# A two-layer graph attention kernel on one core: its row gathers also wait for the query products of the third step behind

## The chip, the cores and the metric

One NeuronCore of a Trainium2 chip runs the whole kernel. The metric is the device time of one execution in microseconds (us). The median of three runs of the kernel before is 5051.74 us, the runs lie between 5045.22 and 5057.14 us.

## The reference, cut to what matters

The input is a graph of 6250 nodes (256 features each) and 200000 edges that are sorted by their destination `dst`. Two layers of graph attention follow one another, each with a residual and a layer norm. In each layer the rows of the source nodes are gathered per edge, a score is formed with the query of the destination node, a softmax runs over all edges of a destination, and the weighted rows are summed per destination.

```python
# layer 0: 4 heads of 32, x[6250,256]; e comes from edge_attr[200000,64]
kj    = k[src] + e
alpha = einsum('ehc,ehc->eh', q[dst], kj) * scale
expa  = exp(alpha - segment_max(alpha, dst)[dst])
alpha = expa / (segment_sum(expa, dst)[dst] + 1e-16)
out   = segment_sum((v[src] + e) * alpha[..., None], dst)
...
# layer 1: one head of 256, with an edge weight added to the score
scores  = sum(q[dst] * k[src], axis=-1) * scale + (edge_weight[:, None] @ we + be)[:, 0]
...
out     = segment_sum(v[src] * attn[:, None], dst)
x       = layer_norm(x + out + linear(x, ws, bs), g1, b1)
```

## The kernel before, in words

The program has five phases with a barrier between them: node projections (n0), the edge phase of layer 0 (L0), node work (n1), the edge phase of layer 1 (L1), node work and the feed-forward part (n2). The change touches the two edge phases alone.

**Steps, pairs, chunks.** The edges are cut into `NS` = 391 steps of 512 edges (4 tiles of 128). Destinations are cut into 49 windows of 128 nodes. A (step, window) combination that has edges is a pair; there are 439, and the program runs 440 (the last is padding). Since the edges are sorted, most steps have one pair, and 48 steps have one more, so a step has 1.12 pairs on average. Eight pairs are a chunk; there are 55. A step's source rows are gathered once and used by all its pairs. Which pair is the first of a step is not fixed at build time: a table `start_tab` that the kernel computes tells, for each step, how many pairs lie ahead of it. POOL loads it eight entries at a time into registers (`load_row`, L264).

**POOL (`gathers`, L622 to L640)** issues the gathers: per step four indirect DMAs, each 128 rows of 1 KB, into one of `SLOTS` = 16 slots of the tile `rows`. Ahead of a step's gathers it waits for three things: that DVE has scored all pairs of all steps up to the fifth behind (`LEAD` = 5, semaphore `score`), that the slot's former rows have been used up (`summed`, that is `msg` in L0 and `agg` in L1), and that the gathers of the step two before have landed. A wait against a register is followed by an increment of a semaphore `gate` (`stand_by`, L61); the two make one instruction, attributed to L67.

**SP** loads the edge attributes (L0) and counts landed steps: `tell_landed` (L490) waits for a pair's gathers and raises `landed`, for which DVE waits in `add_edges` (L1009, layer 0, the first use of the rows) or in `dots` (L1033, layer 1).

**PE** forms, per pair, the edge part (`edge_keys`, operands `w_c` and `ea`, layer 0), the queries of the 512 edges (`queries`, operands in the tile `place`), and, a chunk behind, the weighted sums (`back`: `msg` and `oh` in layer 0, `rows` and `oh` in layer 1). All its matmuls carry the helper's line L1377. Queries lie in two alternating parts of PSUM, so the queries of pair g wait until pair g-2 is scored. PE raises the semaphore `q` once per pair:

```python
after(pe, s["score"], g - 1)                  # L1437: pairs up to g-2 are scored
queries_ready(c, st)
...
if L is L0 or st == 1:
    i.then_inc(s["q"], 1)                     # L1445
...
if st != 1:                                   # bias_products, layer 1
    i.then_inc(s["q"], 1)                     # L1455
```

In layer 1 the signal thus comes behind the four small `bias_products` of the pair (`128x3` outputs). For the third pair of a chunk they stand behind `shrink_first`, the end of the softmax work of the chunk before (L1525 to L1527), while the queries themselves stand ahead of it.

**DVE** scores a pair (`products` L1016 and `scores_of` L1021 in layer 0, `dots` L1033 in layer 1), and does the masked scans, the messages (L1149 in layer 0), its half of the weights (L1154 in layer 1) and the accumulation (L1174) of the chunk before in between. The scans stand at the head of a chunk. **ACT** makes the one-hot operands in `place` (L738, L743) and `oh`, and issues the loads of `dst_row` and of the node blocks (L725, L730).

Of the kernel before, what the change touches and what calls it, by code (L numbers as in the profile page):

```python
# [43 lines left out]
LEAD = 5  # L44
# [10 lines left out]
def after(eng, sem, value):  # L55

    if not (isinstance(value, int) and value <= 0):
        eng.wait_ge(sem, value)


def stand_by(eng, gate, sem, value):  # L61

    if isinstance(value, int):
        after(eng, sem, value)
    else:
        eng.wait_ge(sem, value)
        eng.sem_inc(gate, 1)  # L67


def build(nc, a, out):  # L70
    ctx = ExitStack()
    with ctx:
# [3 lines left out]
        def sem(name):  # L76
            return ctx.enter_context(nc.semaphore(name))
# [186 lines left out]
        def load_row(engine, ap, low=None, top=None, because=None):  # L264

            return nc.values_load_multi_w_load_instructions(ap, engines=[engine], min_val=low, max_val=top,  # L266
                                                            skip_runtime_bounds_check_because=because)[1]
# [13 lines left out]
        def slots(name):  # L281
# [8 lines left out]
                  q=sem("n1_qT"), qc=sem("n1_qT_copied"), qk=sem("n1_qk"), high=sem("n1_high"), low=sem("n1_low"), split=sem("n1_split"))  # L290
# [284 lines left out]
        def _(pool):  # L575
# [44 lines left out]
            gate = sem("pool_gate")  # L620

            def gathers(L):  # L622
                s = L.s
                summed = s["msg" if L is L0 else "agg"]
                starts = {}

                for t in range(NS):
                    if t % 8 == LEAD - 1:
                        k = t - LEAD + 1
                        starts.update(zip(range(k, k + 8), load_row(ENGINE.Pool, start_tab[0:1, k:k + 8], 0, NPAIR)))  # L630
                    if t >= LEAD:
                        stand_by(pool, gate, s["score"], starts[t - LEAD + 1])
                    if t >= SLOTS:
                        stand_by(pool, gate, summed, starts.pop(t - SLOTS + 1))
                    after(pool, s["gathered"][t % 2], 64 * (t // 2))
                    for j in range(JT):
                        pool.indirect_dma_start(  # L637
                            out=L.rows[:, t % SLOTS, j, 0:D], out_offset=None, in_=L.table,
                            in_offset=bass.IndirectOffsetOnAxis(ap=src_all[:, t * JT + j:t * JT + j + 1], axis=0))\
                            .then_inc(s["gathered"][t % 2], 16)  # L640

            def root(norm):
# [6 lines left out]
                return stage  # L649

            gathers(L0)
            end_phase(pool, 2)
            def n1_split(w, b, k):
# [7 lines left out]
            pool.memset(x1_rows[:, :, :, D], 1.0)  # L661
            pool.drain()
            gathers(L1)
            end_phase(pool, 4)

# [1016 lines left out]
```

## Time and profile before

| | us |
|---|---|
| median of three runs | 5051.74 |
| lowest, highest | 5045.22, 5057.14 |
| span of the profiled execution | 6753.4 |
| of it: n0, L0, n1, L1, n2 (windows) | 107, 2998, 303, 2957, 389 |
| busy: PE, DVE, POOL, ACT | 4299.6, 3831.3, 3308.1, 3003.4 |

The profiled execution has only its span; no time of its own beside it is given. It is 1702 us longer than the median of the runs without the profiler. A row of instructions reads: start, duration, engine, line, operation, tile written <- tiles read, and in brackets how long the engine was idle before it and what ended that. "remote" or "another core or an unknown queue" is a wait whose releaser the profile does not name. A busy time holds instructions alone; between two gathers POOL is not counted as busy.

### The profile page before, as it was taken

The page shows a single profiled execution, that of the slowest core. Times are in us where ns is not written, and L with a number is a line of the kernel's source. Part 1 is how long each engine was busy: PE and PEld are TensorE (multiplying, and loading weights), DVE is VectorE, ACT ScalarE, POOL GpSimd, SP SyncE. Part 2 cuts the span into 40 slices and gives each one's busy share as a digit, 9 for nine tenths or more (in the row PEclk, how much of TensorE's full clock was granted, in tenths as well). Part 3 has the DMA queues.
Part 4 walks back from the last instruction along what each step waited for, and adds up shares of the span by engine and source line. Part 5 has one row for each costly group of instructions (what it writes and reads, how often), then busy time and mean ns, then how long its engine had stood idle before and what let it go on. Part 6 is the DMA issues. An engine that isn't in the chain of part 4 may idle for free.

```text
span 6753.4 us, 105844 instructions
## 1 busy us (share of the span) xinstructions
PE 4299.6 (64%) x23291; PEld 3492.8 (52%) x23291; DVE 3831.3 (57%) x12902; ACT 3003.4 (44%) x6997; POOL 3308.1 (49%) x3637
## 2 busy tenths in 40 slices
PE   6555555565565566566746666666666666666698
PEld 3454554555455555454534555555554555554587
DVE  4565665666566666666734444455454444444588
ACT  1444454555454454554324444444444444444432
POOL 2545555455555455452355545554555554454355
PEclk8777777777777777777978778787888787777899
DMA  6555555555555555553446556565666665555422
GB/s 201 148 145 148 146 145 146 145 153 148 149 152 145 145 152 154 148 148 99 122 141 163 161 153 162 157 162 157 164 160 158 160 160 158 157 163 158 125 73 70
DMA packets 774181, 996.11 MB, mean 147 GB/s; under 512 B 189569, under 2 KB 559489, under 8 KB 773553
## 3 DMA queue, kind: packets, MB, share of 16 engines
q10 hardware_dynamic: 394272, 443.81, 23.8%
q0 software_dynamic: 150224, 410.39, 22.7%
q1 hardware_dynamic: 229056, 135.14, 7.5%
q8 instruction: 198, 3.24, 0.2%
q14 instruction: 431, 3.52, 0.2%
HBM read 862.98 MB, written 125.90 MB: 146 GB/s over the span
## 4 chain that ended last, share of the span: by engine, by line
another core or an unknown queue 22%; PE 21%; DVE 17%; issue 16%; DVEq 7%; ACTq 5%; ACT 5%; DMA 2%; POOL 2%; SPq 1%; POOLq 1%
PE ps L1377 20%; DVE rows L1009 2%; DVE score L1021 2%; DVE prod L1033 2%; ACT oh L750 2%; DVE acc L1174 2%; DMA acc_d<-acc 2%; ACT place L738 1%; ACTq L827 1%; DVE prod L1016 1%; DVEq L1233 1%; ACTq L730 1%; SPq L266 1%; DVEq L1231 1%
## 5 line engine op out<-in xcount | busy, mean ns | idle before, releaser
L637 POOL DMA_INDIRECT rows<-kv_d,src_all x1564 | 1535.2, 982 | 1543.1 <-DVE score L1021 951.0
L637 POOL DMA_INDIRECT rows<-x_d,src_all x1564 | 1487.0, 951 | 1450.5 <-DVE prod L1033 962.3
L1377 PE MATMUL ps<-place 128*128 128x256 bf16 (+2 forms) x10560 | 1459.9, 288 | 296.4 <-issue 186.8
L1377 PEld LDWEIGHTS ps<-place 128*128 128x128 bf16 (+1 forms) x10560 | 1250.9, 149 | 587.4 <-issue 317.6
L1377 PE MATMUL ps<-rows,oh 128*128 x3520 | 1093.2, 470 | 457.3 <-DVE oh L1154 340.7
L1033 DVE SCALAR_TENSOR_TENSOR prod<-rows,ps 128x256 f32<-128x256 f32 x1760 | 637.3, 418 | 906.8 <-remote 549.9
L1377 PEld LDWEIGHTS ps<-rows,oh 128*128 128x128 f32 x3520 | 797.8, 236 | 617.9 <-issue 478.8
L750 ACT ACTIVATE oh<-iota_row,rel 128x128 f32<-128x128 f32 x2640 | 837.9, 388 | 552.9 <-remote 408.8
L1377 PE MATMUL ps<-msg,oh 128*128 128x132 f32 x3520 | 607.0, 330 | 595.8 <-DVE msg L1149 331.8
L1377 PEld LDWEIGHTS ps<-msg,oh 128*128 128x128 f32 x3520 | 544.1, 235 | 638.9 <-DVE msg L1149 421.0
L738 ACT ACTIVATE place<-dst_row,node_tab 128x512 f32<-128x512 int32 (+1 forms) x880 | 613.2, 708 | 385.4 <-DVE acc L1174 145.3
L757 ACT ACTIVATE oh<-oh,prob,prob_neg 128x128 f32<-128x128 f32 x880 | 374.2, 484 | 801.7 <-remote 466.4
L743 ACT ACTIVATE place<-place,ones 128x512 f32<-128x512 f32 (+1 forms) x880 | 635.0, 722 | 184.7 <-issue 115.5
L1009 DVE TENSOR_TENSOR rows<-rows,ps 128x1024 f32 x440 | 537.3, 1221 | 176.8 <-issue 95.9
L1377 PE MATMUL ps<-w_c,ea 128*128 128x256 f32 x1760 | 610.4, 482 | 34.9 <-issue 23.5
L1016 DVE TENSOR_TENSOR prod<-rows,ps 128x512 f32<-128x512 f32 x440 | 299.8, 681 | 555.3 <-remote 503.3
L1174 DVE SCALAR_TENSOR_TENSOR acc<-acc,keep_tab,ps 128x132 f32<-128x132 f32 (+1 forms) x770 | 318.7, 414 | 508.2 <-remote 279.3
L1377 PEld LDWEIGHTS ps<-w_c,ea 128*128 128x128 f32 x1760 | 391.6, 246 | 89.7 <-issue 26.2
L789 ACT ACTIVATE pen_r<-ps 128x128 f32<-128x128 f32 (+1 forms) x110 | 30.0, 272 | 813.6 <-remote 337.8
L1021 DVE TENSOR_REDUCE score<-prod 128x16 f32<-128x512 f32 x440 | 301.9, 686 | 44.7 <-issue 10.8
L1149 DVE TENSOR_TENSOR msg<-rows,prob 128x512 f32<-128x512 f32 x440 | 293.3, 687 | 1.6 <-issue 1.3
L762 ACT ACTIVATE oh<-oh,ones 128x1024 f32<-128x1024 f32 x275 | 268.9, 978 | 19.2 <-issue 0.3
(217 smaller groups left out, 4152.9 us busy)
## 6 DMA issues: line engine op xcount, KB each, us to landing
dst_row<-in_dst_row ACTq DMA_DIRECT2D x880, 256.0 KB
place<-q_d ACTq DMA_DIRECT2D x440, 192.8 KB
acc_d<-acc ACTq DMA_DIRECT2D x440, 128.5 KB
ea<-in_ea SPq DMA_DIRECT2D x440, 128.0 KB
acc_d<-acc ACTq DMA_DIRECT2D x440, 66.0 KB
place<-q_d ACTq DMA_DIRECT2D x440, 64.0 KB
rows<-kv_d,src_all POOLq DMA_INDIRECT x1564
rows<-x_d,src_all POOLq DMA_INDIRECT x1564
```

Of the source, the lines that this page charges most:

```text
L637: pool.indirect_dma_start(out=L.rows[:, t % SLOTS, j, 0:D], out_offset=None, in_=L.table, in_offset=bass.IndirectOffsetOnAxis(ap=src_all[: ...
L738: act.activation(L.oht[st % PLACES], dst_row[st % PLACES][:, :], ACT.Abs, scale=-1.0, bias=node_tab[:, bass.ds(g, 1)])
L743: act.activation(L.oht[st % PLACES], L.oht[st % PLACES], ACT.Relu, scale=-1.0, bias=ones[:, 0:1])\
L750: act.activation(oh[:, st % OHS, j, :], iota_row[:, :], ACT.Abs, scale=-1.0, bias=rel[par][:, st, j:j + 1])
L757: i = act.activation(o, o, ACT.Relu, scale=prob_neg[par][:, n:n + 1], bias=prob[par][:, n, 0:1])
L1009: v.tensor_tensor(kv, kv, e_ps(b).rearrange("p (j n) -> p j n", j=JT).unsqueeze(2) .to_broadcast([P, JT, 2, DM]), ALU.add).then_inc(s["add ...
L1016: v.tensor_tensor(half, held(kv_rows, slot[CH * c + st])[:, :, 0:DM], q_ps(L, st % 2).rearrange("p (j n) -> p j n", j=JT), ALU.mult)
L1021: v.tensor_reduce(score[par][:, st * JT:(st + 1) * JT, :], prod[:, :, st % 2 * DM:(st % 2 + 1) * DM] .rearrange("p j (h n) -> p j h n", h= ...
L1033: i = v.scalar_tensor_tensor(out=prod[:, j, :], in0=x1[:, j, 0:D], scalar=1.0, in1=q_ps(L, b)[:, j * D:(j + 1) * D], op0=ALU.mult, op1=ALU ...
L1149: v.tensor_tensor(m, held(kv_rows, slot.pop(g))[:, :, DM:2 * DM].rearrange("p j (h c) -> p j h c", h=HEADS), prob[par][:, st * JT:(st + 1) ...
L1174: v.scalar_tensor_tensor(acc[st % ACCS][:, 0:L.AW], old[:, 0:L.AW], keep_tab[:, bass.ds(g, 1)], agg_ps(L, b), ALU.mult, ALU.add).then_inc( ...
L1377: return pe.matmul(out_, lhsT=lhsT, rhs=rhs, start=first, stop=last)
```

## The change: one more wait ahead of each step's gathers

From step 5 on, POOL also waits until `q` has reached the number of pairs that lie ahead of step t-2, that is, until PE has signalled the query products of all pairs of all steps up to t-3. The wait stands between that for `score` and that for the slot. So that the table entry t-2 is in a register by then, each block of eight entries is loaded two steps earlier.

```diff
                 for t in range(NS):
-                    if t % 8 == LEAD - 1:
-                        k = t - LEAD + 1
+                    if t >= LEAD - 3 and (t - LEAD + 3) % 8 == 0:
+                        k = t - LEAD + 3
                         starts.update(zip(range(k, k + 8), load_row(ENGINE.Pool, start_tab[0:1, k:k + 8], 0, NPAIR)))
                     if t >= LEAD:
                         stand_by(pool, gate, s["score"], starts[t - LEAD + 1])
+                        stand_by(pool, gate, s["q"], starts[t - LEAD + 3])
                     if t >= SLOTS:
                         stand_by(pool, gate, summed, starts.pop(t - SLOTS + 1))
                     after(pool, s["gathered"][t % 2], 64 * (t // 2))
```

On POOL, at steps 3 to 7 of layer 0, the order before. A row `L637 DMA ... [waits ...]` is the first gather of a step with the semaphores waited for since the row ahead; the row behind it holds the other three gathers. `l0_gathered0` and `l0_gathered1` are the landings of even and odd steps.

```order
L637 DMA rows<-kv_d,src_all 128x256 [waits l0_gathered1]
L637 DMA rows<-kv_d,src_all 128x256 x3
L266 TENSOR_LOAD start_tab
L266 ISA x16
L637 DMA rows<-kv_d,src_all 128x256 [waits l0_gathered0]
L637 DMA rows<-kv_d,src_all 128x256 x3
L637 DMA rows<-kv_d,src_all 128x256 [waits l0_score,l0_gathered1]
L637 DMA rows<-kv_d,src_all 128x256 x3
L637 DMA rows<-kv_d,src_all 128x256 [waits l0_score,l0_gathered0]
```

And the order after the change, on POOL at steps 2 to 6 (the gathers' line is now L638):

```order
L266 TENSOR_LOAD start_tab
L266 ISA x16
L638 DMA rows<-kv_d,src_all 128x256 [waits l0_gathered0]
L638 DMA rows<-kv_d,src_all 128x256 x3
L638 DMA rows<-kv_d,src_all 128x256 [waits l0_gathered1]
L638 DMA rows<-kv_d,src_all 128x256 x3
L638 DMA rows<-kv_d,src_all 128x256 [waits l0_gathered0]
L638 DMA rows<-kv_d,src_all 128x256 x3
L638 DMA rows<-kv_d,src_all 128x256 [waits l0_score,l0_q,l0_gathered1]
L638 DMA rows<-kv_d,src_all 128x256 x3
L638 DMA rows<-kv_d,src_all 128x256 [waits l0_score,l0_q,l0_gathered0]
```

The table load moved two steps up and `l0_q` stands in each later step; no gather changed its place among the others, and the other engines' programs are the same.

## Rows read from the trace of the kernel before

**Rows 1.** The page's first two lines: span, and busy time of each engine.
```profile
span 6753.4 us, 105844 instructions
...
PE 4299.6 (64%) x23291; PEld 3492.8 (52%) x23291; DVE 3831.3 (57%) x12902; ACT 3003.4 (44%) x6997; POOL 3308.1 (49%) x3637
```
**Rows 2.** The page's chain of waits, shares of the span by engine.
```profile
another core or an unknown queue 22%; PE 21%; DVE 17%; issue 16%; DVEq 7%; ACTq 5%; ACT 5%; DMA 2%; POOL 2%; SPq 1%; POOLq 1%
```
**Rows 3.** Busy time by phase: window, length, each engine's busy time, clock, DMA share, GB/s.
```profile
0.00:107.00 107.00, 82.96 (x246) 46.22 (x246) 59.47 (x199) 11.37 (x28) 13.60 (x67) 0.97 0.77 228
107.00:3105.00 2998.00, 1729.37 (x9137) 1516.66 (x9138) 1832.43 (x3947) 1493.61 (x3452) 1535.17 (x1564) 0.75 0.54 148
3105.00:3408.00 303.00, 207.15 (x993) 151.03 (x991) 204.28 (x903) 110.84 (x363) 79.51 (x148) 0.88 0.36 101
3408.00:6365.00 2957.00, 1949.46 (x10944) 1490.27 (x10945) 1426.00 (x6804) 1269.09 (x2824) 1487.01 (x1564) 0.80 0.59 159
6365.00:6754.00 389.00, 330.71 (x1976) 288.58 (x1973) 309.10 (x1052) 118.52 (x331) 192.80 (x294) 0.96 0.24 71
```
**Rows 4.** The page's costliest groups: busy, mean ns, idle before and its releaser.
```profile
L637 POOL DMA_INDIRECT rows<-kv_d,src_all x1564 | 1535.2, 982 | 1543.1 <-DVE score L1021 951.0
L637 POOL DMA_INDIRECT rows<-x_d,src_all x1564 | 1487.0, 951 | 1450.5 <-DVE prod L1033 962.3
...
L1033 DVE SCALAR_TENSOR_TENSOR prod<-rows,ps 128x256 f32<-128x256 f32 x1760 | 637.3, 418 | 906.8 <-remote 549.9
```
**Rows 5.** POOL on the tile rows: gathers' ns min/median/max, and who ended POOL's idle time.
```profile
L637 POOL DMA_INDIRECT rows<-kv_d,src_all x1564: 942/949/1462, 107.4 to 3099.0; - x196
...
  DVE prod L1033: 962.3, 259
  DVE score L1021: 951.0, 183
...
  DVE msg L1149: 7.8, 1
```
**Rows 6.** Timeline of POOL in L1: last gather of step 161, first three of step 162.
```profile
4609.27 0.95 POOL L637 DMA_INDIRECT rows<-x_d,src_all  x1 [0.30 <-issue]
4616.64 0.95 POOL L637 DMA_INDIRECT rows<-x_d,src_all  x1 [6.42 <-DVE prod L1033]
4617.89 0.94 POOL L637 DMA_INDIRECT rows<-x_d,src_all  x1 [0.30 <-issue]
```
**Rows 7.** Timeline of DVE in L1: last dot of pair 176, first of 178, first of 182.
```profile
4615.33 0.42 DVE L1033 SCALAR_TENSOR_TENSOR prod<-rows,ps 128x256 f32<-128x256 f32 x1
...
4628.34 0.42 DVE L1033 SCALAR_TENSOR_TENSOR prod<-rows,ps 128x256 f32<-128x256 f32 x1 [5.66 <-remote]
...
4650.86 0.42 DVE L1033 SCALAR_TENSOR_TENSOR prod<-rows,ps 128x256 f32<-128x256 f32 x1 [5.55 <-remote]
```
**Rows 8.** Timeline of PE in L1: queries of 178, shrink, then bias products of 178.
```profile
4618.89 1.95 PE L1377 MATMUL ps<-place 128*128 128x256 bf16 x12 [0.93 <-ACT place L743]
...
4622.73 0.58 PE L1377 MATMUL ps<-shrink_d,first_oh 1*128 1x1 f32 x2 [1.45 <-issue]
4623.25 2.94 PE L1377 MATMUL ps<-place 128*128 128x3 bf16 x20
```
**Rows 9.** Timeline in L0: score 203, POOL's step 186, messages, queries of 205, use in pair 209.
```profile
1530.18 0.69 DVE L1021 TENSOR_REDUCE score<-prod 128x16 f32<-128x512 f32 x1
...
1531.75 0.95 POOL L637 DMA_INDIRECT rows<-kv_d,src_all  x1 [3.81 <-DVE score L1021]
...
1532.85 0.68 DVE L1149 TENSOR_TENSOR msg<-rows,prob 128x512 f32<-128x512 f32 x1
1533.00 1.35 POOL L637 DMA_INDIRECT rows<-kv_d,src_all  x1 [0.30 <-issue]
...
1533.42 1.39 PE L1377 MATMUL ps<-place 128*128 128x128 f32 x8
...
1557.63 1.22 DVE L1009 TENSOR_TENSOR rows<-rows,ps 128x1024 f32 x1 [0.29 <-issue]
```
**Rows 10.** Direct DMAs of the size of one gather: KB each, us from issue to landing.
```profile
rows<-x_d SPq DMA_DIRECT2D x98, 128.0 KB, 2.1
...
kv_d<-rows ACTq DMA_DIRECT2D x49, 128.0 KB, 2.8
```
**Rows 11.** POOL's register waits (line L67): ns min/median/max.
```profile
L67 POOLq EVENT_SEMAPHORE  x1522: 4/17/737, 138.9 to 6338.6; - x191
```

## The prediction

> **What bounds the kernel now.** I read the page's span and busy times first. The span is 6753.4 us, and no engine is busy for more than 64% of it [rows 1]. That span is 1701.7 us above the median of 5051.74 us. The chain of waits puts 22% of the span, 1486 us, on a releaser that the profile cannot name [rows 2]. It is of the size of the difference. In layer 1 such pauses show as DVE idle for 5.66 and 5.55 us before its dots, ended by "remote" [rows 7]. I take them to be mostly a matter of the profiled execution, so the trace is slower than the kernel that is timed, and a margin read from it must be cut down.
>
> The windows by phase come next [rows 3]. Outside the edge phases lie 107 + 303 + 389 = 799 us. If these are the same without the profiler, each edge phase takes about (5052 - 799) / 2 = 2127 us there, which is 2127 / 391 = 5.44 us per step and 2127 / 440 = 4.83 us per pair.
>
> Then POOL. Inside a step, gathers start 1.25 us apart (4616.64 and 4617.89), of which 0.30 is a gap that is not counted as busy [rows 6]. With that gap, POOL needs 1535 + 1564 x 0.30 = 2004 us in L0 and 1487 + 469 = 1956 us in L1 [rows 3, 4]. PE needs 1949 us in L1 and DVE 1832 us in L0 [rows 3]. So POOL, half idle by the page, is the most loaded engine of both phases: 3960 of 4254 us in a run without the profiler. It has 294 us to spare over 782 steps, 0.38 us a step. In the trace nearly all its waiting is for DVE's scores (183 times in L0, 259 in L1) and once for a slot [rows 5]; it is held back by its lead of five steps.
>
> **The change, part by part.**
> - *Added instructions.* 386 waits in each phase, 772 in all. The present kind has a median of 17 ns, and there are 1522 = 2 x (386 + 375) of them [rows 11]. All of them exposed would be 13 us. But POOL's sequencer passes them beside the gather that runs. I count them only where POOL is idle when it comes to them, 442 steps [rows 5], 7.5 us at most; and as that idle time itself is mostly spare, I take 3 us.
> - *The table load.* It moves by two steps, its count stays. SP, PE, ACT and DVE have the same programs. Nothing.
> - *The wait itself.* It is never weaker than the old one. The queries of pair g are signalled only once pair g-2 is scored, and step t-3 ends at least two pairs behind the end of step t-5. So the gathers come later in nearly every step that is now held by a score. By how much, from one place in each phase:
>   - L1, step 162. The score of pair 176 ends at 4615.75 [rows 7] and POOL starts 0.89 us later, at 4616.64 [rows 6]. The queries of pair 178, the last of step 159, are done at 4620.84, but its signal comes with the first bias products from 4623.25 on [rows 8]. With 0.89 us of reaction the gathers would start at about 4624.1, 7.5 us later.
>   - L0, step 186. POOL starts at 1531.75, after the score of pair 203. The queries of pair 205 end at 1533.42 + 1.39 = 1534.81 [rows 9]. The start would be at 1535.7, 3.9 us later.
> - *Who waits for it.* Behind the gathers stands SP's count of landed steps, then DVE. The fourth gather is issued 3 x 1.25 = 3.75 us after the first. The trace has no landing time for a gather. Direct DMAs of its size land 2.1 to 2.8 us after issue [rows 10], and I take 2.8. In L1 the rows would be there at 4624.1 + 6.6 = 4630.7, and are first used at 4650.86 [rows 7], 20 us later. In L0 they would be there at 1542.3 and are used at 1557.63 [rows 9], 15 us later.
> - *Without the profiler.* The pauses are worth 1701.7 / 880 = 1.9 us per pair. In L1 four pairs lie between, 20 - 8 = 12 us are left; in L0 it is six pairs at most, 15 - 12 = 3 us left. A second way: two whole steps lie between the signal and the first use, 2 x 5.44 = 10.9 us. Of these 0.9 + 3.75 + 2.8 = 7.5 us are needed, and 3.4 us are left. So the lead that is taken away was spare, in the mean. A gap of more than some 3 us on PE just ahead of a signal would use it up.
> - *DVE and POOL side by side.* In L0 a gather takes 982 ns in the mean, against 951 in L1 [rows 4], with a median of 949 and a maximum of 1462 [rows 5]. The one of 1.35 us at 1533.00 ran while DVE made messages [rows 9]. The excess over L1 is 1564 x 0.031 = 48 us of POOL's time. A shift by 3.9 us in a pair period of 4.8 us may move gathers onto such instructions or off them. With nothing lengthened POOL gains 48 us; I take 0, as the gathers of a step fill nearly the whole period anyway (4 x 1.25 = 5.0 of 5.44 us).
>
> The Trainium skill, page "SBUF — State Buffer", section "Who interferes with whom", says that a DVE instruction with two SBUF inputs contends with a GpSimd instruction that reads SBUF, and that DMAs as such never contend with a compute engine. The messages have both inputs in SBUF, so the trace agrees with it. By the page the sum would be open by these 48 us in L0, and unchanged in L1.
>
> The sum: 0 + 3 + 0 = 3 us on 5051.74, about 5055.
>
> **The rivals.**
> - *The lead is spare* (forecast). For it: the margins of 3 to 12 us, and POOL's single wait for a slot. It gives 5042 to 5062.
> - *POOL has no time to lose* (slower). POOL has 0.38 us to spare a step. At the head of a chunk DVE and PE do the scans, and the signal of the chunk's third pair stands behind them in layer 1. POOL now sits idle there instead of working ahead, and has to make up for it later at 5.0 us a step against a demand of 5.44, which it cannot do within a chunk of seven steps (7 x 0.38 = 2.7 us) if it loses more than that. It decides where the delay exceeds the 3.4 us that are left. The L0 place exceeds it by 0.5 us, the L1 place by 4.1 us. One such loss in each of the 55 heads of a phase gives 55 x 0.5 = 28 us up to 55 x 4.1 = 226 us. I take 40 us, near the low end, since in the traced L1 place DVE still met its rows 20 us early: 5092. Against it: the same margins.
> - *A better phase* (faster). The gathers now start when PE has its operands, so they are less in the way of loads and of DVE's messages. From 15 us (a third of the excess) to 48 us: 5004 to 5037, I take 5030. For it: POOL is the most loaded engine, so what it gains counts. Against it: nothing shows that the new phase is better than the old. The page's rule named above is this rival's mechanism for layer 0.
> - *The change does nothing*: if POOL lags so far behind without the profiler that no gate ever holds it, both gates are met when it comes to them. 5052. For it: 3960 of 4254 us. Against it: 442 steps held by a score in the trace.
>
> **How the numbers follow.** About 0.2% (10 us) is what a measurement of this kernel can tell from no change. Spare lead 0.37, nothing 0.04, no time to lose 0.36, better phase 0.23. Same: the first two, 0.41. Slower 0.36, faster 0.23. The predicted time is 5055, the likeliest case. The range goes down to 5020, half into the better phase, and up to 5095, a little past my value for the slower rival; about 2 in 10 are left out, mostly above it. As the cases of both signs hold more than the likeliest, its own range stands here too: 5042 to 5062.
>
> **What the profile after would show.** If I am right: POOL's idle time before gathers is ended mostly by PE instead of DVE. Its total is the same within a few per cent, since it issues the same work. DVE's waits on SP (the landed count) don't grow, and the mean gather stays near 982 and 951 ns. If the slower rival holds, DVE's first use of the rows (L1009, L1033) is released by SP more often, at the second to fourth pair of a chunk. If the faster one holds, the mean gather of L0 falls towards 951 ns, or DVE's and PE's waits on the loads shrink. The forecast is wrong if the time leaves 5042 to 5062 us.

## The result: a little slower, 5078.25 us against 5055.24

Seven runs of each kernel were timed on one chip.

| | us |
|---|---|
| before, median (lowest to highest, 7 runs) | 5055.24 (5045.22 to 5063.39) |
| after, median (lowest to highest, 7 runs) | 5078.25 (5066.89 to 5087.49) |
| ratio, 95% interval | 1.0042, 1.003 to 1.0055 |
| profiled execution of after: its time, its span | 5078.96, 5077.2 |

The change costs 0.42%, some 21 us. That is more than the 0.2% that a measurement can tell, and it lies outside the 5042 to 5062 us that I gave to my forecast.

The first surprise is the profiled execution itself. The span of before was 1702 us above its timed runs [rows 1]. The one of after lies 1.8 us below its own time and amid its timed runs. So the profiler doesn't slow this kernel. Before was therefore profiled once more, unchanged, and gave a span of 5059.5 us. I call this the **clean trace** of before, and the one that the prediction read the **paused trace**. All comparisons up to the last experiment are with the clean one.

The page's first two lines of the clean trace of before:

```profile
span 5059.5 us, 105844 instructions
...
PE 3809.0 (75%) x23291; PEld 3120.8 (62%) x23291; DVE 3808.2 (75%) x12902; ACT 3002.8 (59%) x6997; POOL 3302.1 (65%) x3637
```

And of after, with its chain of waits and its two groups of gathers:

```profile
span 5077.2 us, 106616 instructions
...
PE 3828.2 (75%) x23291; PEld 3135.5 (62%) x23291; DVE 3810.1 (75%) x12902; ACT 3001.0 (59%) x6997; POOL 3289.3 (65%) x3637
...
PE 20%; DMA 17%; DVE 15%; ACT 13%; ACTq 13%; issue 13%; DVEq 5%; POOL 3%; POOLq 1%; SPq 0%
...
L638 POOL DMA_INDIRECT rows<-kv_d,src_all x1564 | 1514.1, 968 | 751.4 <-issue 411.9
L638 POOL DMA_INDIRECT rows<-x_d,src_all x1564 | 1490.0, 953 | 606.2 <-issue 433.0
```

No engine is busy for more than 75%, and 22% on an unnamed releaser [rows 2] is gone. The clean trace of before has these two groups with 1532.0 and 1484.3 us, and idle times of 719.5 and 596.5 us. The idle time before gathers thus rose from 1316.0 to 1357.6 us, by 3%. Of both numbers some 938 us are the 3128 gaps of 0.30 us, so what lies above the gaps rose from 378 to 419 us.

Where the time went, by windows that are cut at the first gather and the last accumulation of each edge phase. The clean before (window, length, busy time of PE, PEld, DVE, ACT, POOL, clock, DMA share, GB/s):

```profile
108.00:2317.00 2209.00, 1557.87 (x9295) 1335.20 (x9295) 1843.17 (x4015) 1509.68 (x3520) 1532.01 (x1564) 0.88 0.73 201
2317.00:2575.00 258.00, 177.26 (x833) 124.82 (x833) 173.87 (x833) 86.62 (x294) 79.52 (x148) 0.92 0.40 114
2575.00:4704.00 2129.00, 1684.50 (x11055) 1345.75 (x11055) 1442.09 (x6875) 1289.56 (x2860) 1484.27 (x1564) 0.92 0.82 221
```

After:

```profile
107.00:2327.00 2220.00, 1562.03 (x9295) 1340.20 (x9295) 1842.62 (x4015) 1508.37 (x3520) 1514.06 (x1564) 0.88 0.73 200
2327.00:2585.00 258.00, 178.56 (x833) 125.81 (x833) 176.49 (x833) 86.75 (x294) 78.88 (x149) 0.91 0.40 114
2585.00:4721.00 2136.00, 1698.00 (x11055) 1354.22 (x11055) 1441.46 (x6875) 1288.88 (x2860) 1489.94 (x1564) 0.91 0.84 221
```

L0 is 11 us longer and L1 is 7 us longer; n1 between them is the same. DVE and ACT are busy for the same time or a little less. POOL is busy 18 us less in L0 and 6 more in L1, PE 4 and 14 us more, at a granted clock that is 0.88 in L0 both times. So the loss of L0 is waiting, not work. The clean trace of before also shows how little POOL had to spare: 1532 + 1564 x 0.30 = 2001 of 2209 us in L0.

Who ends POOL's idle time. In the clean before (us, times):

```profile
  issue: 894.4, 2798
...
  DVE score L1021: 168.3, 129
  DVE prod L1033: 101.4, 89
...
  PE ps L1377: 29.6, 58
```

In the kernel after:

```profile
  issue: 845.7, 2635
  PE ps L1378: 333.1, 315
...
  DVE msg L1150: 38.8, 50
...
  DVE score L1022: 17.4, 57
  DVE prod L1034: 11.7, 37
```

These counts are not steps. They hold the ordinary gaps of 0.30 us inside a step too, when an update of such a semaphore happened to fall into one. Counted at the first gather of each step alone, a score ended the idle time at 117 steps in the clean before (239 us; 78 in L0 and 39 in L1), and at 356 steps in the paused trace, where the prediction reads 442 [rows 5]. After the change PE ends it at 141 steps (280 us; 82 in L0 and 59 in L1), and a score at 13 (4 us). In layer 1 the slot's semaphore is raised by PE too: the clean before has 22 such steps, so not all of the 59 are the new wait's.

The first question was whether the rows now come late. I took, for each step behind the fifth, the time from the end of its last gather to DVE's first use of its rows:

| from last gather to first use, us | L0 median (shortest) | L1 median (shortest) |
|---|---|---|
| paused trace of before | 20.2 (8.4) | 29.3 (18.0) |
| clean trace of before | 11.7 (4.0) | 16.4 (2.1) |
| after | 7.9 (2.4) | 8.4 (2.0) |

The change takes 3.8 us in L0 and 8.0 us in L1, as forecast (3.9 and 7.5). A step's last gather packet ends behind its last gather's instruction by a median of 2.7 us in L0 and 3.3 us in L1 in the clean before (2.4 and 3.3 after), and by 3.7 us in L0 and 4.6 us in L1 or more in one step of twenty. So the typical step still has its rows some 5 us early after the change, but the shortest times of the table leave nothing. DVE's waits on SP's landed count, of which late rows are a part, rose from 25.3 + 52.9 to 28.3 + 57.6 us over the program, by 8 us.

### The profile page after: what moved, and what is told of

Its sections match the earlier page's. It is cut to its first block, busy times and chain, and to the rows that moved or that the text cites. A ratio compares the mean times of both kernels' runs of the same rounds, so it can differ in the third digit from the quotient of the medians.

```text
span 5077.2 us, 106616 instructions
## 1 busy us (share of the span) xinstructions
PE 3828.2 (75%) x23291; PEld 3135.5 (62%) x23291; DVE 3810.1 (75%) x12902; ACT 3001.0 (59%) x6997; POOL 3289.3 (65%) x3637
## 3 DMA queue, kind: packets, MB, share of 16 engines
q14 instruction: 436, 3.57, 0.2%
## 4 chain that ended last, share of the span: by engine, by line
PE 20%; DMA 17%; DVE 15%; ACT 13%; ACTq 13%; issue 13%; DVEq 5%; POOL 3%; POOLq 1%; SPq 0%
PE ps L1378 18%; DMA acc_d<-acc 15%; ACT oh L751 7%; ACTq L828 4%; ACT place L739 3%; ACTq L731 3%; DVE rows L1010 3%; ACTq L726 3%; POOL rows L638 2%; DVE score L1022 2%; DVE acc L1175 2%; DVE prod L1034 1%; DMA dst_row<-in_dst_row 1%; DVEq L1234 1%; ACT place L744 1%
## 5 line engine op out<-in xcount | busy, mean ns | idle before, releaser
L638 POOL DMA_INDIRECT rows<-kv_d,src_all x1564 | 1514.1, 968 | 751.4 <-issue 411.9
L638 POOL DMA_INDIRECT rows<-x_d,src_all x1564 | 1490.0, 953 | 606.2 <-issue 433.0
L1378 PE MATMUL ps<-place 128*128 128x256 bf16 (+2 forms) x10560 | 1313.7, 274 | 144.5 <-DVE score L1022 65.0
L1378 PEld LDWEIGHTS ps<-place 128*128 128x128 bf16 (+1 forms) x10560 | 1154.8, 140 | 370.9 <-issue 89.0
L1378 PE MATMUL ps<-rows,oh 128*128 x3520 | 916.7, 411 | 127.3 <-issue 116.3
L1378 PEld LDWEIGHTS ps<-rows,oh 128*128 128x128 f32 x3520 | 683.7, 202 | 230.2 <-issue 134.6
L1378 PE MATMUL ps<-msg,oh 128*128 128x132 f32 x3520 | 506.1, 290 | 231.4 <-DVE msg L1150 129.8
L1378 PEld LDWEIGHTS ps<-msg,oh 128*128 128x128 f32 x3520 | 439.1, 194 | 290.3 <-DVE msg L1150 270.9
L1378 PE MATMUL ps<-w_c,ea 128*128 128x256 f32 x1760 | 541.7, 437 | 25.3 <-DMA ea<-in_ea 21.2
L1378 PEld LDWEIGHTS ps<-w_c,ea 128*128 128x128 f32 x1760 | 346.7, 219 | 68.5 <-issue 22.1
```

What stands on the lines that cost most here:

```text
L638: pool.indirect_dma_start(out=L.rows[:, t % SLOTS, j, 0:D], out_offset=None, in_=L.table, in_offset=bass.IndirectOffsetOnAxis(ap=src_all[: ...
L1378: return pe.matmul(out_, lhsT=lhsT, rhs=rhs, start=first, stop=last)
```

## The experiments

At this point there were three explanations: the added instructions cost their issue time; the rows come late; or POOL, held at the head of a chunk, makes up for it later and its gathers then meet other transfers. Against them stood the chance that all of it is noise of the single traces. The first two groups of kernels were timed against before on a chip each, with 25 and 17 runs of before (medians 5055.62 and 5053.36 us). Spans of single traces scatter by some 10 us, so times are compared by the ratios of the timed runs.

### One more wait of the old kind (e1)

```diff
                         stand_by(pool, gate, s["score"], starts[t - LEAD + 1])
+                        stand_by(pool, gate, s["q"], starts[t - LEAD + 1])
```

The 772 waits are added with a bound that the score's wait implies already, and the table load stays.

> The kernel before with one more register wait per step on the query semaphore, with the value of the score wait (steps up to t-5), so that it is always met once the score is. It has the added instructions and none of the added delay. Theory A (the later start of the gathers costs the time): 5055 us, no change within 0.1%. Theory C (the 772 added instructions cost it): the whole 0.42%, 5076 us.

Measured: 5059.78 us, ratio 1.0012 (1.0001 to 1.0024). The instructions alone cost about 0.12%, 6 us, with an upper end of 12. My term was 3 us with a bound of 13. The traces show why 17 ns was too little for one of them: two such waits stand 0.096 us apart on POOL's sequencer even where both are met, and POOL starts a median of 0.97 us behind the score that frees it in e1, 0.87 in the clean before.

### The change in one layer (e2, e3)

```diff
+                        stand_by(pool, gate, s["q"], starts[t - LEAD + 3]) if L is L0 else None
```

with the table load moved as in the change; in e3 the condition is `L is L1`.

> The new wait in the edge phase of layer 0 alone. Theory A (POOL has too little time to spare for being held later): both phases pay, layer 0 with the shorter delay (3.9 us at the place read) pays less: 5055 + 5 to 10 us. Theory B (the shifted gathers meet other DMAs, above all the stores of the sums, whose landings now stand in 15% of the chain of waits): layer 0 moves less (203 GB/s against 225 in layer 1), so nearly nothing: 5055 to 5059 us.

> The new wait in the edge phase of layer 1 alone. Theory A: most of the loss, 5055 + 13 to 18 us, as the signal of a chunk's third pair is late there by 7.5 us at the place read. Theory B: nearly all of it, 5055 + 19 to 23 us. Theory C: half of it, 11 us, as half of the instructions are here. Together with the run for layer 0 it tells whether the two parts add up to the whole.

Measured: layer 0 alone 5072.99 us, ratio 1.0037 (1.0024 to 1.005); layer 1 alone 5063.76 us, ratio 1.002 (1.0009 to 1.003). The two add up to 0.57% against 0.42% for both, which their intervals allow. Layer 0 seems to carry the larger part, in the traces too (11 of 18 us), though its delay is half that of layer 1; the two intervals overlap. The delay alone is then no measure of the cost. POOL is as loaded in one layer as in the other, 2001 of 2209 us in L0 and 1953 of 2129 in L1, but DVE has 1843 us of work in L0 against 1442.

### The query wait in place of the score wait (e4)

```diff
-                        stand_by(pool, gate, s["score"], starts[t - LEAD + 1])
+                        stand_by(pool, gate, s["q"], starts[t - LEAD + 3])
```

> The kernel after without the old wait for the scores; the query wait alone is at least as strict, since the queries of pair g come after the score of pair g-2. The gathers start when they do in the kernel after, with as many instructions as before. Theory A or B (the later start costs the time): about 5070 us, +0.3%. Theory C (instructions; the implied wait alone measured +0.12%): that part goes, and what is left is +0.3%. If the instructions were all of it: 5055 us.

Measured: 5072.1 us, ratio 1.0036 (1.0023 to 1.0048), with as many instructions as before (105844). So the later start costs by itself, and it is most of the 0.42%.

### One step tighter (e6)

The wait is for all pairs of all steps up to t-2, and the table load moves up by one more step.

```diff
+                        stand_by(pool, gate, s["q"], starts[t - LEAD + 4])
```

> The query wait one step tighter: all steps up to t-2. The gathers start one more step (about 5 us) later. In the trace after, the first use of the rows stands a median of 5.6 us (layer 0) and 8.5 us (layer 1) behind the end of the last gather, and landing takes some 1.5 to 3 us of it. Theory A: now the rows are late in most steps, DVE's waits on the landed count grow from 86 us to several hundred, and the time is 5200 us or more. Theory B: no such waits at the third step, and a further loss of the same size as before, 5095 us, if the rows still come in time.

(For layer 0 the table above has 7.9 us from the last gather to the first use, not 5.6.)

Measured: 5343.59 us, ratio 1.0591 (1.0575 to 1.0606). Here the rows are late. From the list of waits (engine, tile, line <- releaser: us, times, longest) first the clean before, then this kernel:

```profile
DVE prod L1033 <- SPq L495: 52.9, 42, 10.1
```

```profile
DVE prod L1034 <- SPq L495: 460.6, 205, 11.0
...
DVE rows L1010 <- SPq L495: 315.3, 228, 5.5
```

DVE waits for the landed count for 776 us instead of 78, and the kernel is 290 us slower. That is what late rows look like. After the change the same two lines hold 86 us. So late rows are at most a small part of the 21 us.

### Another lead with the old wait alone (e7, e8)

`LEAD = 6` and `LEAD = 4` in the kernel before.

> The kernel before with LEAD = 6: one step more of lead. In the second trace of before POOL is held by a score in 218 of 782 steps for 270 us. If every bit of lead is worth something, this is the mirror image of the change: -0.1 to -0.3%, 5040 to 5050 us. If the lead of five steps is already spare, no change; if gathers that run further ahead meet more of the other DMAs, slower.

> The kernel before with LEAD = 4: the wait is for the scores of all steps up to t-4 instead of t-5, no query wait, no added instruction. The gathers start about one step later than before where a score holds them, a little earlier than in the kernel after. If the lead is what counts, whichever semaphore takes it away: +0.1 to +0.3%, 5060 to 5070 us. If it is the binding to PE's signal: no change, 5055 us.

Measured: LEAD = 6 5054.01 us, ratio 1.0001 (0.9992 to 1.0011); LEAD = 4 5075.35 us, ratio 1.0048 (1.0035 to 1.0061). More lead than five brings nothing, and one step less costs as much as the change. The lead of before was just enough, not more than enough.

### What the traces of this set show together

DVE's waits before the accumulation for the landing of a store of `acc`, and before the first use of the rows, in L0. The rows are from the list of waits of each trace, over L0. The clean before:

```profile
DVE acc L1174 <- DMA acc_d<-acc: 109.0, 51, 3.5
DVE rows L1009 <- SPq L495: 25.3, 32, 11.6
```

Layer 0 alone (e2):

```profile
DVE acc L1175 <- DMA acc_d<-acc: 132.9, 55, 3.8
DVE rows L1010 <- SPq L495: 24.8, 19, 10.7
```

LEAD = 4 (e8):

```profile
DVE acc L1174 <- DMA acc_d<-acc: 95.2, 52, 4.7
DVE rows L1009 <- SPq L495: 51.9, 59, 2.8
```

| L0 | query wait there | DVE for `acc_d`, us | DVE for rows, us |
|---|---|---|---|
| before, e1, e3, e7 | no, or met at once | 109.0, 110.9, 104.9, 106.2 | 25.3, 24.8, 24.9, 24.7 |
| after, e2, e4 | yes | 120.7, 132.9, 124.3 | 28.3, 24.8, 27.1 |
| e8 | no, lead of four | 95.2 | 51.9 |

Four traces without the new wait in L0 lie within 6 us of each other, and all three with it wait 10 to 28 us longer for a store to land. (The traced run of e2, with 132.9, was its slowest, 5094.29 us.) LEAD = 4 loses its time at another place: its rows are late. So a shorter lead can cost at either place.

Where in a chunk? DVE's own time tells it for L0. I cut it at the end of each pair's score and took the mean of the stretches over the chunks. The stretch up to the seventh score is 6.04 to 6.21 us long in the four traces without the wait and 6.35 to 6.55 us in the three with it; the one up to the sixth is 4.43 to 4.45 and 4.49 to 4.51 us. All others agree within 0.04 us. Before against after that is 0.14 + 0.08 us a chunk, some 12 us over the chunks, about the 11 us by which L0 is longer. DVE's busy time in them is the same. All but a few of L0's waits for a store stand in the stretch up to the seventh score, at one accumulation, the sixth of the chunk, which needs the landing of the chunk's second store. In the stretch up to the sixth score DVE waits for rows: 0 to 0.9 us in all in the four traces, 2.6 to 3.9 in the three. So in L0 the time goes to that store for the most part, and to late rows for a small one.

POOL's busy share with its gaps, by the pair of the chunk in L0, is 0.84 at the second pair before and 0.63 after. It is 0.94, 0.95 and 0.89 at the last three before and 0.98, 0.97 and 0.94 after. POOL stands at the head of the chunk, and runs without a pause at its end. There the accumulations and their stores lie. One chunk shows it. POOL and DVE in the timeline of the clean before (the rows between the two blocks, further gathers and other work of DVE, are not shown):

```profile
1238.80 0.94 POOL L637 DMA_INDIRECT rows<-kv_d,src_all  x1 [4.59 <-DVE score L1021]
```

```profile
1258.08 0.35 DVE L1174 SCALAR_TENSOR_TENSOR acc<-acc,keep_tab,ps 128x132 f32<-128x132 f32 x1
1260.75 0.35 DVE L1174 SCALAR_TENSOR_TENSOR acc<-acc,keep_tab,ps 128x132 f32<-128x132 f32 x1 [2.33 <-DMA acc_d<-acc]
```

and the same chunk after:

```profile
1239.62 0.95 POOL L638 DMA_INDIRECT rows<-kv_d,src_all  x1 [4.12 <-PE ps L1378]
```

```profile
1260.18 0.35 DVE L1175 SCALAR_TENSOR_TENSOR acc<-acc,keep_tab,ps 128x132 f32<-128x132 f32 x1
1263.93 0.35 DVE L1175 SCALAR_TENSOR_TENSOR acc<-acc,keep_tab,ps 128x132 f32<-128x132 f32 x1 [3.41 <-DMA acc_d<-acc]
```

The store's wait is 1.08 us longer at this place. The median time from issue to landing of the 440 stores of L0 is 3.29 us in the clean before, 3.29 in e1, 3.30 in e3 and 3.23 in e7; it is 3.32 after, 3.46 in e2 and 3.41 in e4, and 3.19 in e8. For the chunk's second store alone, the one that is waited for, the mean is 3.38 to 3.53 us without the new wait and 3.62 to 3.82 with it (3.57 in e8). In the clean before, the 17 stores with fewer than 20 gather packets begun in the 3 us behind their issue land in 1.66 us in the median, those with 60 to 100 in 3.58. That goes with stores that land later beside gathers. But nearly all of the 17 are the last stores of the phase, where the phase's loads run out too, so the gathers are not singled out.

The Trainium skill, page "DMA: Bandwidth & Descriptors", section "Queues, rings and completion order", says that a DMA's semaphore increment lands only after every earlier write of the same DMA engine, across its queues. The landing times beside gathers are what it leads one to expect, since stores and gathers have different queues; no run here tests it.

This is read from traces and has not been shown by taking the cause away. For layer 1 the stores don't explain it. DVE's waits for `acc_d` there are 114.1 us before and 99.1 after, and those for rows 52.9 and 57.6. e3 has 67.2 for rows. By the pair of the chunk the rows tell one thing: ahead of a chunk's eighth pair DVE waits for them 5.4 to 9.3 us in all in the four traces without the wait in L1 (before, e1, e2, e7), and 11.3 to 17.7 us in the three with it (after, e3, e4). That is of the size of L1's 7 us, but other waits of DVE scatter by as much between these traces, so it is not shown to be the cause.

### More buffers for the stores (f1 to f4)

To take the cause away, `ACCS` was raised from 4 to 8, so that DVE waits for a store that lies eight pairs back (f1 before, f2 after). In f3 and f4 the stores are counted in four semaphores in place of two as well, so that ACT, too, waits for an older one.

```diff
-ACCS = 4
+ACCS = 8
...
-        acc_scaled = sb("acc_scaled", [P, D + 1])
+        acc_scaled = zero_rows
```

f3 and f4 also have:

```diff
-            for x in ("gathered", "stored"):
+            for x in ("gathered",):
...
+        L0.stored = [(n0["store"][b], 48 * turns(b)) for b in range(4)]
+        L1.stored = [(n1["store"][b], 32 * turns(b)) for b in range(4)]
...
-                    after(act, s["stored"][b], 16 * (CH // 2 * c + st // 2))
-                    act.dma_start(window(L.acc_d, g), acc[st % ACCS][:, 0:L.AW]).then_inc(s["stored"][b], 16)
+                    after(act, stored, base + 16 * (CH // 4 * c + st // 4))
+                    act.dma_start(window(L.acc_d, g), acc[st % ACCS][:, 0:L.AW]).then_inc(stored, 16)
...
```

The parts left out make DVE's wait and SP's wait at the end of the phase use the same four semaphores.

> The kernel before with eight buffers for the sums instead of four (the space comes from one tensor less, zero_rows is used twice). DVE then waits for a store eight pairs old instead of four, so its 221 us of waits for acc_d stores go to about 0. ACT still issues a store only when the store two pairs before has landed. If DVE's waits are on the path: faster, 4900 to 5000 us. If ACT's own wait is what holds the chain and DVE's only mirrors it: no change, 5055 us.

> The kernel after with the same eight buffers. Theory B1 (the shifted gathers delay the stores' landings and DVE pays for it, +12 to +24 us in layer 0 in the traces): the change costs only the instructions here, +0.1% against the run with eight buffers before. Theory A (rows late, POOL short of time), or B2 (the cost comes through ACT's store wait): the change costs 0.3 to 0.5% here too.

> The kernel before with eight buffers and four store semaphores: ACT issues a store once the one four pairs before has landed, instead of two. Now neither DVE nor ACT should wait for a store. If the stores' landings bound the kernel at all, this is the fastest so far, 4850 to 5000 us; POOL, busy for 93 to 98% of most pairs, then becomes the limit, at 391 x 2 x 5.0 us and the 797 us outside, about 4800 us. If POOL already is the limit, no change.

> The kernel after with the same two edits. Theory B (any form of store wait is how the change costs time): +0.1% against the same edits before. Theory A: with the stores out of the way DVE and ACT run closer behind POOL, POOL has no time to spare, and holding it at the head of a chunk costs as much as before or more, +0.4% and up.

The measurement went another way than any of these. In this job every run of the unchanged kernel before took 6740.7 to 6790.8 us (23 runs, median 6767.22), with the pauses of its first profile; so the four kernels can be compared with each other only.

| | us | ratio to before |
|---|---|---|
| f1: before, 8 buffers | 6759.11 | 0.9993 (0.998 to 1.0006) |
| f2: after, 8 buffers | 6194.27 | 0.9151 (0.9124 to 0.9178) |
| f3: as f1, four store semaphores | 6753.7 | 0.9983 (0.9967 to 0.9999) |
| f4: as f2, four store semaphores | 6191.5 | 0.9156 (0.9132 to 0.9179) |

The question on the stores is not answered. The buffers and semaphores do next to nothing here (f1, f3), where pauses take up much of the time. But the change itself is worth 8.4% in this condition (f2/f1 0.9164, f4/f3 0.9168), against a loss of 0.42% in the other. The experiments e1 to e3 had run on the same chip in the clean condition. So it belongs neither to the profiler nor to a chip; what sets it is open.

### What the pauses are

From the trace of f1, the page's first line and who ended POOL's idle time on the tile rows:

```profile
span 6752.5 us, 105836 instructions
```

```profile
  DVE prod L1033: 947.5, 255
  DVE score L1021: 931.4, 171
```

The same two views of f2:

```profile
span 6192.5 us, 106608 instructions
```

```profile
  PE ps L1378: 1081.3, 324
...
  remote: 351.8, 139
```

By these lines POOL waits for 1879 us in f1 and for 1433 us in f2. Counted at the first gather of each step it is held by a score at 341 steps in f1, and by PE or an unnamed releaser at 450 in f2, so f2 is held more often and for a shorter time.

A pause from near, in the paused trace of before, in the timeline, a little ahead of [rows 9]: POOL's gathers, PE's products, then DVE and ACT.

```profile
1524.49 0.94 POOL L637 DMA_INDIRECT rows<-kv_d,src_all  x1 [0.30 <-issue]
1525.74 0.95 POOL L637 DMA_INDIRECT rows<-kv_d,src_all  x1 [0.30 <-issue]
1527.00 0.94 POOL L637 DMA_INDIRECT rows<-kv_d,src_all  x1 [0.30 <-issue]
```

```profile
1524.78 1.05 PE L1377 MATMUL ps<-place 128*128 128x128 f32 x8
1525.67 1.07 PE L1377 MATMUL ps<-msg,oh 128*128 128x132 f32 x8
1530.24 1.02 PE L1377 MATMUL ps<-msg,oh 128*128 128x132 f32 x5 [3.50 <-DVE acc L1174]
```

```profile
1529.74 0.35 DVE L1174 SCALAR_TENSOR_TENSOR acc<-acc_scaled,keep_tab,ps 128x132 f32<-128x132 f32 x1 [3.65 <-remote]
```

```profile
1529.74 1.28 ACT L750 ACTIVATE oh<-iota_row,rel 128x128 f32<-128x128 f32 x4 [5.54 <-remote]
```

PE ended its products of the edge part, the queries and the sums at 1524.94, 1525.84 and 1526.74. The trace has the updates of the three semaphores at 1529.77, 1529.87 and 1529.71, 3 to 5 us later. DVE and ACT go on with them. The gathers that POOL had issued from 1518.23 to 1527.00 moved their last packet at 1529.43. So all engines stood while the updates were out and gathers were landing, and went on when these were done.

Over the whole trace, the time from an instruction's end to the next update of its semaphore, PE's instructions split by whether gather packets were moving at that end (waits over 12 us are left out, as updates are missing from the records of the paused traces: 355 of 440 of the queries' in L0):

| share of PE's updates that come 2 us or more late | before, paused | f2, paused | before, clean |
|---|---|---|---|
| while gather packets move | 63% of 1498 | 55% of 1655 | 0% of 2337 |
| otherwise | 14% of 1549 | 13% of 1406 | 0% of 970 |

It isn't PE alone. Where no gather packet begins in the 0.5 us behind the instruction, 7% of PE's updates are late, 2% of DVE's, 2% of ACT's and 1% of POOL's; with 20 to 40 packets it is 64%, 40%, 45% and 34%. The packets of queue 1 make no such difference for PE (41% without, 41% with 20 to 40), those of queue 10 a smaller one (26%, 51%). In the clean trace an update comes 0.01 us behind its instruction in the median, with gathers beside it or not.

It reads as if in the paused condition semaphore updates stood behind the traffic of the gathers, so that a gather would hold up the engines that it runs beside. This is a correlation in two traces, not shown by an experiment. It fits the gain: the query's signal comes 4.13 us late in the mean in L0 before, and 3.04 in f2 (2.62 and 2.36 in L1). How the wait shortens these delays isn't shown. My first idea, shorter runs of gather packets, is not what f2 has: their median length, with gaps of up to 0.3 us joined, is 2.41 us against 1.27.

## Why the prediction was right or wrong

- **What bounds the kernel.** "POOL, half idle by the page, is the most loaded engine": right. The clean trace has 2001 of 2209 us in L0 and 1953 of 2129 in L1 by the same sum.
- **The pauses.** This premise failed: "I take them to be mostly a matter of the profiled execution". They are a condition in which unprofiled runs of before take 6767 us as well. In the clean condition the profiled execution costs nothing that shows. My correction of the margins by 1.9 us per pair rests on that premise. It left 12 us in L1 and 3 in L0, and the second way 3.4; the trace of after has medians of some 5 us in both layers.
- **The delays.** 3.9 and 7.5 us from one place in each layer; the medians are 3.8 and 8.0.
- **The readings of the rows.** The 442 steps "held by a score" are gaps and not steps; it was 356. The "single wait for a slot" is that of layer 0. In layer 1 PE raises the slot's semaphore, and the paused trace has 12 waits that PE ended, 61.8 us. Neither changes the sum.
- **The instructions.** 3 us, measured 6 (0.1 to 12), by e1. The 17 ns that I priced one at is its own duration; it takes up 0.096 us.
- **The delay is hidden.** Cost zero ("the lead that is taken away was spare, in the mean"). This is the step by which 5055 missed 5078: without any added instruction (e4) the later start costs 0.36%, 18 us. I asked only whether the rows come before their use in the mean. They nearly always do, yet DVE waits longer for the stores of `acc` in L0, and in both layers somewhat longer for rows late in a chunk. I had looked at one transfer behind POOL's wait, and not at those beside which its work now falls.
- **DVE and POOL side by side.** Zero, between plus 48 and minus 48. The mean gather of L0 fell from 980 ns (clean) to 968, so gathers took 18 us less; in L1 they took 6 us more. None of the gain shows in the time. It is the step that the "better phase" rested on: its mechanism came, and its gain did not.
- **The rivals.** "POOL has no time to lose" has the sign, and much of the mechanism: POOL idles at the head of the chunk and makes up for it later. Its price was 28 to 226 us with 40 taken, against 21 measured. It named DVE's first use of the rows as the new wait, and that grew by 8 us in all; the wait for the stores grew by 12 in L0. It placed the late rows at the second to fourth pair of a chunk; in L1 they grew at the eighth. "The change does nothing" was wrong: PE ends the idle time at 141 steps.
- **The signs.** POOL's waits ended mostly by PE, yes. Total idle the same within a few per cent, yes (3%). DVE's waits on SP not growing, nearly. The mean gather of L0 fell to 968 ns, which was a sign of the faster rival. I had no sign for the stores. The last sign, a time outside 5042 to 5062 us, came, and by it the forecast was wrong although most of its other signs came true.
- **The range.** 5020 to 5095 holds the result, but only because it was drawn wide enough for the slower rival. The mechanism that I forecast didn't bring the time there, so that is luck as far as "the lead is spare" goes. Against the second condition no number of the prediction stands: there the change, with eight buffers, makes the kernel 8.4% faster. With its own four buffers it was not run there.

## What to carry to other kernels

A lead that is just enough has no spare part, even where every row still arrives in time. Before a prefetch is started later, ask what it will then run beside: here the engine that is 90% loaded by issue makes up for lost time at the end of a chunk, where a store is waited for. A count of waits is not a count of held steps: count at the one instruction that can be held. Where a profiled span lies far from the timed runs, profile once more before reasoning from it, since the difference may be a condition of the chip, in which the same edit has the other sign.

## What the runs showed of the hardware that was not expected

- The same kernel, on the same chip at different times, takes 5055 or 6767 us. In the slower condition all four kernels of the job showed it, and the granted clock was 0.79 in place of 0.91 for before, and 0.82 for f2. PE's updates were 2 us or more late in 63% of the cases beside moving gathers.
- A store of 66 KB that is issued beside gathers takes 3.3 us to land in the median, and 1.7 at the end of the phase, where hardly any gather packets move.
- POOL's gathers were lengthened beside DVE even in the clean trace: 184 of 1564 in L0 lasted over 1 us, 1.23 us in the mean, and 169 of these overlapped the making of messages. In L1, 34 did. The Trainium skill, page "SBUF — State Buffer", section "Who interferes with whom", leads one to expect this of an instruction with two SBUF inputs, and L0's messages are one. The same section infers that such a `tensor_tensor` doesn't hold up the generation of descriptors. Here the 417 gathers that overlapped a message took 1.07 us in the mean and all others 0.95. The accumulations overlapped 142 of the 184 too.
- A register wait with its increment reads 17 ns, but two in a row stand 0.096 us apart on POOL's sequencer, in the clean before, in e1 and after.
- What the second condition is, why the chunk's second store lands later in L0, and what the loss in layer 1 consists of, stay open.
